# Twenty-five indirect fetches moved from the end of an attention stage into its loop over key tiles

## The reference, cut to what matters

```python
h = jnp.maximum(_layernorm(x, axis=-1), 0.0)
x = x + _L0_gnn_ref(h, qW, kW, vW, src, dst)      # attention over edges, 4 heads
h = jnp.maximum(_layernorm(x, axis=-1), 0.0)
# _L1_gnn_ref: x[tgt] is the row of the edge's own target
gamma = e / denom[tgt]                            # softmax of edge_weight per target
msg = jax.nn.relu(x[tgt] @ Wv + bv) * gamma[:, None]
out = jax.ops.segment_sum(msg, tgt, num_segments=n)
```

## Time and profile before

| what | value |
|---|---|
| median of 3 runs | 1339.63 us (1333.62 to 1341.48) |
| span of the profiled execution | 1334.5 us, 23321 instructions |
| PE busy | 1089.8 us, 82% |
| DVE busy | 974.4 us, 73% |
| ACT busy | 691.7 us, 52% |
| POOL busy | 599.0 us, 45% |
| attention, first to last POOL operation | 414.8 to 865.9 us |

### The profile page before, as it was taken

One profiled execution on the slowest core, in us unless ns is written; L12 is line 12 of the kernel. 1 busy time (PEld: TensorE's weight loads), 2 busy tenths in 40 slices (PEclk: granted clock), 3 DMA queues, 4 the chain that ended last, 5 costly groups with the idle time before them and its releaser, 6 DMA issues.

```text
span 1334.5 us, 23321 instructions
## 1 busy us (share of the span) xinstructions
PE 1089.8 (82%) x8345; PEld 633.6 (47%) x8345; DVE 974.4 (73%) x1600; ACT 691.7 (52%) x903; POOL 599.0 (45%) x343
## 2 busy tenths in 40 slices
PE   3878787787796888888788888837996999999893
PEld 2555554454461222222222222214696987788783
DVE  8677888886575999999999999918556535422466
ACT  7555565555446998999898999800000000000221
POOL 8532533422005998999999989960000000000000
PEclk9888878879796999999999999968997999999996
DMA  0100000000144111111112222110011000000201
GB/s 10 30 33 5 7 7 5 8 17 1 40 129 114 36 44 45 47 48 44 45 35 60 53 51 49 45 44 1 1 37 39 25 14 1 22 14 4 66 28 36
DMA packets 98907, 44.80 MB, mean 34 GB/s; under 512 B 85196, under 2 KB 96716, under 8 KB 98672
## 3 DMA queue, kind: packets, MB, share of 16 engines
q1 hardware_dynamic: 97104, 41.58, 11.8%
q0 software_dynamic: 1696, 1.74, 0.5%
HBM read 30.73 MB, written 12.56 MB: 32 GB/s over the span
## 4 chain that ended last, share of the span: by engine, by line
PE 50%; DVE 25%; issue 11%; ACT 5%; POOL 5%; DMA 2%; another core or an unknown queue 2%; SPq 1%; DVEq 0%; ACTq 0%; POOLq 0%
PE PS L1324 19%; DVE Eb L1150 15%; PE PS L553 10%; PE PS L557 8%; POOL Eb L982 3%; DVE Eb L1144 3%; PE PS L1709 3%; PE PS L1332 2%; ACT Eb L1115 2%; PE PS L1074 2%; PE PS L1064 1%; PE PS L1315 1%; ACT Eb L1117 1%; ACT Eb L1119 1%
## 5 line engine op out<-in xcount | busy, mean ns | idle before, releaser
L982 POOL TENSOR_SCALAR Eb<-Eb 128x1024 f32<-128x1024 f32 (+4 forms) x175 | 431.1, 2485 | 74.1 <-ACT Eb L1119 72.8
L1150 DVE SCALAR_TENSOR_TENSOR Eb<-Eb,PS 128x1024 f32<-128x1024 f32 (+4 forms) x350 | 366.7, 1084 | 16.7 <-ACT Eb L1117 10.5
L1324 PE MATMUL PS<-hs,CT 128*128 128x192 f16 (+3 forms) x2500 | 263.3, 267 | 4.0 <-DVE B L1557 1.8
L1119 ACT ACTIVATE Eb<-PS,small 128x1024 f32<-128x1024 f32 (+2 forms) x263 | 251.5, 997 | 28.0 <-PE PS L1064 24.5
L593 ACT ACTIVATE CT<-PS 128x500 f32 x313 | 183.7, 587 | 142.9 <-PE PS L557 135.1
L553 PE MATMUL PS<-mov,oneS 128*128 128x100 f16 x1565 | 184.6, 231 | 76.1 <-issue 71.0
L1324 PEld LDWEIGHTS PS<-hs,CT 128*128 128x128 f16 (+1 forms) x2500 | 227.5, 99 | 37.7 <-DVE SG L1557 2.7
L553 PEld LDWEIGHTS PS<-mov,oneS 128*128 128x128 f16 x1565 | 146.6, 107 | 157.9 <-issue 113.8
L1064 PE MATMUL PS<-Qb,Kb 96*128 96x512 f16 (+3 forms) x700 | 182.8, 364 | 11.1 <-ACT Eb L1119 7.2
L1074 PE MATMUL PS<-Eb,V 128*25 128x512 f32 (+3 forms) x1400 | 169.9, 558 | 3.4 <-DVE Eb L1150 1.8
L435 DVE TENSOR_TENSOR oneS<-iotaX,KL 128x2560 f16<-128x2560 int16 x80 | 120.1, 1501 | 71.6 <-PE PS L557 69.0
(11 more groups left out here) (258 smaller groups left out, 1006.6 us busy)
## 6 DMA issues: line engine op xcount, KB each, us to landing
Kb<-kd SPq DMA_DIRECT2D x168, 96.0 KB, 2.4
qd<-QH SPq DMA_DIRECT2D x12, 192.0 KB, 2.7
kd<-QH SPq DMA_DIRECT2D x12, 192.0 KB, 3.1
hs<-t_d SPq DMA_DIRECT2D x12, 192.0 KB, 2.5
Qb<-qd SPq DMA_DIRECT2D x4, 384.0 KB, 3.9
CT<-x_d SPq DMA_DIRECT2D x1, 1200.0 KB, 7.6
x_d<-B SPq DMA_DIRECT2D x6, 192.0 KB, 1.9
t_d<-A SPq DMA_DIRECT2D x6, 192.0 KB, 1.8
```

The costliest lines, as they stand in the source:

```text
L982: g.tensor_scalar(e, e, ELO, None, ALU.max).then_inc(S("floored"), 1)
L1119: a.activation(e, ps, ACT.Exp, scale=K.unsc[0:r, :]).then_inc(S("score_read"), 1)
L1150: v.scalar_tensor_tensor(out=e, in0=e, scalar=EHI, in1=cn, op0=ALU.min, op1=ALU.mult).then_inc(S("weighed"), 1)
L1324: m = p.matmul(bank(t % FIRST)[0:r, 0:w], K.CT[:, a, 128 * t:128 * t + r], hs[:, a, :, :].rearrange("p k d -> p (k d)"), start=(a == 0), s ...
```

## The change

`attn_gpsimd` waits for `last_edge` at its head. A fetch is then issued behind POOL's operation of steps 9, 15, 21, ... 153 (tiles 0 to 24 of `gG`), in place of the blocks of 4 at the stage's end and of 8 and 13 in the next. The semaphores and the waits of the readers stay as they were.

```diff
+GAMMA_AT = {6 * t + 9: t for t in range(NT)}
+
+
 def attn_gpsimd(g, K):
     S = K.S
+    g.wait_ge(S("last_edge"), 1)
+
+    def gamma(t):
+        i = [t < b for a, b in X_IN].index(True)
+        g.indirect_dma_start(out=K.gG[:, t:t + 1], out_offset=None, in_=K.gs_d,
+                             in_offset=bass.IndirectOffsetOnAxis(ap=K.endI[:, t:t + 1], axis=0)
+                             ).then_inc(S("gamma_in%d" % i), 16)
+
     for it in range(len(ITS)):
...
                 g.tensor_scalar(e, e, ELO, None, ALU.max).then_inc(S("floored"), 1)
+        if it in GAMMA_AT:
+            gamma(GAMMA_AT[it])
     g.wait_ge(S("floored"), halves("P", len(ITS)))
-    g.wait_ge(S("last_edge"), 1)
-    gammas(g, K, 0)
-
-
-def gammas(g, K, i):
-
-    for t in range(*X_IN[i]):
-        g.indirect_dma_start(out=K.gG[:, t:t + 1], out_offset=None, in_=K.gs_d,
-                             in_offset=bass.IndirectOffsetOnAxis(ap=K.endI[:, t:t + 1], axis=0)
-                             ).then_inc(K.S("gamma_in%d" % i), 16)
...
 def prop_gpsimd(g, K):
     S = K.S
-    gammas(g, K, 1)
-    gammas(g, K, 2)
     for i, (a, b) in enumerate(X_IN):
         g.wait_ge(S("gamma_in%d" % i), 16 * (b - a))
```

## The result

The changed kernel takes 1354.12 us, the median of four runs (1345.97 to 1358.65), the kernel before 1339.03 (four runs, 1333.62 to 1341.48). The ratio is 1.0107, 95% interval 1.0065 to 1.0148: slower by about 1%. 1352.6 us was forecast. The profiled execution of the changed kernel is the fastest of its four, 1345.97 us with a span of 1344.0; so the profiles differ by 9.5 us, the medians by 15.1. The forecast of 13.0 lies between.

The account below looks back on a forecast made before the run. The prediction took POOL and DVE together to bound the attention, with two late hand-overs at the propagation's start. 26.7 - 13.7 = +13.0 us on the median of 1339.6 gave 1352.6 us, range 1338 to 1368.

Parts of the forecast that it names:

- The attention, +26.7: Attention: the 25 fetches, paid in POOL's order, add 26.7 us, with ends of 13 and 38.
- ten steady slots: Attention: ten fetches in stretches where POOL has no gap, 1.5 us each, 15.0 us.
- six of blocks 4 and 5: Attention: six fetches in the steady part of blocks 4 and 5, 1.35 us each, 8.1 us.
- nine near a block's start: Attention: nine fetches close to a block's start, partly swallowed by POOL's gaps, 0.4 us each, 3.6 us.
- The 0.2 us that I put on top for line 1144: Attention: a fetch without a gap costs 1.5 us, not 1.30, as POOL's next operation is stretched by line 1144.
- The meeting I described: Attention: POOL's delayed operation begins inside DVE's line 1144 and takes 3.19 us, 0.43 more than 2.76.
- The stage change, -13.7: From attention to propagation: without the fetches 13.7 us go, 12.1 of late hand-overs and 1.6; ends 0 and 15.3.
- The 12.1 us of hand-overs: Propagation's start: two late hand-overs from PE, to ACT 6.33 and to DVE 5.77 us, go with the fetches.
- The clock's share, 1.6 us: Propagation's start: PE stays warmer at granted clock 1.00, so its first group is 1.6 us shorter.
- 1, that the hand-overs stay: Propagation's start: the late hand-overs have another cause and remain; 1366.3 us, chance 0.25.
- 2, that POOL's idle time swallows more: Attention: POOL's idle time of about 20 us takes up more of the fetches; 1338.4 us, chance 0.16.
- 3, that 1144 and POOL exclude each other: Attention: the fetch or POOL's next operation lasts until line 1144 ends; attention +38, 1363.9 us, chance 0.09.

Follow-up runs that it names:

- experiment 2: The changed kernel with each fetch one step earlier, behind even steps: 1381.08 us, ratio to before 1.0307.
- experiment 8: The changed kernel with a second, spare fetch behind each of the first 24: 1400.66 us, ratio to before 1.0457.
- 1: No fetch at all, against the kernel before: a memset writes 1.0 into gG instead; 1325.96 us, ratio 0.9895.
- 3: The 25 fetches moved to POOL's idle time: 17 in the projection, 6 at the attention's head, 2 behind steps 32 and 82; 1338.09 us, ratio to before 0.9977.
- 4: The changed kernel plus 21 spare fetches into unused columns at the propagation's head: 1369.54 us, ratio to before 1.0233.
- 5: The changed kernel plus 21 spare fetches in the propagation, held back until `lin_read`: 1377.79 us, ratio to before 1.0265.
- 7: The changed kernel plus 21 spare fetches at the propagation's head, 14 tiny memsets behind each, some 3.4 us apart: 1352.29 us, ratio to before 1.0093.
- 9: The kernel before with four tiny memsets ahead of each of the propagation's 21 fetches, 1.80 us apart: 1324.89 us, ratio 0.9889.
- 10: The kernel before with two tiny memsets ahead of each of the propagation's 21 fetches, 1.49 us apart: 1324.76 us, ratio 0.9895.
- 12: The kernel before with six tiny memsets ahead of every third fetch of the propagation: 1325.65 us, ratio 1.0005 to before at 1325.27.
- run 6: The 25 fetches placed singly: 6 in the projection, 2 at the attention's head, 17 at steps beside POOL's gaps; 1337.36 us, ratio to before 0.9972.

## Why the prediction was right, and where not

*What bounds the kernel.* Right: POOL and DVE are bound together, a fetch in POOL's order is paid in full, and neither catches up. The chain's swap from DVE to POOL is the same statement.

*The attention, +26.7.* Measured +24.3. For each slot, the time from the start of POOL's operation three steps ahead to that three steps behind (the last slot reaches to the end of the attention), less the same in before:

| kind | forecast | measured |
|---|---|---|
| ten steady slots | 15.0 (1.5 each) | 12.9 (0.75 to 2.21; six of them 1.24 to 1.29) |
| six of blocks 4 and 5 | 8.1 (1.35 each) | 6.8 (-0.47 to 1.92) |
| nine near a block's start | 3.6 (0.4 each) | 4.6 (-1.15 to 2.25) |

The lower bound held: 1.30 forecast from the earlier trace rows, 1.25 found. The 0.2 us that I put on top for line 1144 was wrong for the steady slots. The meeting I described does happen, but the price falls on the other engine. The timeline of DVE behind the first fetch:

```profile
443.22 1.69 DVE L1147 TENSOR_SCALAR Eb<-Eb 128x1024 f32<-128x1024 f32 x1
444.94 3.54 DVE L1153 SCALAR_TENSOR_TENSOR Eb<-Eb,PS 128x1024 f32<-128x1024 f32 x3
448.86 1.22 DVE L1153 SCALAR_TENSOR_TENSOR Eb<-Eb,PS 128x1024 f32<-128x1024 f32 x1 [0.38 <-POOL Eb L993]
450.00 0.69 DVE L1147 TENSOR_SCALAR Eb<-Eb 128x1024 f32<-128x1024 f32 x1
```

Line 1147 starts 0.08 us ahead of POOL's next operation and takes 1.69 us, not 0.69; POOL's takes its usual 2.77. DVE pays 1.00 us within the 1.25 that POOL is late anyway, and has to wait for POOL 0.38 us a step later. So the 1.00 us lies in DVE's slack and costs nothing. In experiments 2 and 8 it comes to 1.42 us (2.11 less 0.69) behind a POOL operation that is already late, and there it is paid.

*The stage change, -13.7.* Measured -14.9. The 12.1 us of hand-overs are gone, and 1, 3, 4, 5, 7, 9 and 10 show that the fetches made them, with the caution told under 12. The clock's share, 1.6 us, was wrong as a mechanism. Windows of the kernel after, from the first group's copy to the second group's product (columns as in the earlier trace rows):

```profile
907.64:909.93 2.29, 1.57 (x13) 1.15 (x10) 0.00 (x1) 0.69 (x2) 0.00 (x0) 1.00 0.00 0
909.93:914.08 4.15, 0.00 (x0) 0.00 (x0) 3.94 (x18) 0.21 (x1) 0.00 (x0) 0.74 0.00 0
914.08:917.88 3.80, 3.11 (x13) 2.61 (x14) 3.56 (x17) 0.59 (x1) 0.00 (x0) 0.50 0.00 0
```

The granted clock is 1.00 (2.4 GHz) at the first product, which takes 1.15 us in place of 2.02. Then PE stands idle for 4.15 us while DVE normalises the next rows, as in the kernel before, and the clock falls to 0.50 (1.2 GHz). The second group's transposes, product and source sums take 1.10, 2.03 and 6.45 us, and the group 11.9 us (914.08 to 925.99) in place of 11.2: 0.9 gained and 0.7 lost, nearly nothing together. The prediction overlooked that idle stretch.

A gain of 2.7 us that nobody forecast fills the place: the first transposes end 18.8 us behind POOL's last operation (889.29 to 908.09) and not 21.5 (865.93 to 887.39). It can't be put down to the fetches. The five other kernels without a fetch at this place (1, 2, 3, 6, 8) have 19.6 to 21.1, as much as the kernel with two memsets (21.0), which has them. So kernels with no fetch there at all lie 2.3 us apart, and what sets this stretch no run shows. That the term of 13.7 comes so near to 14.9 is in part luck.

*The sum.* By the profiles 24.3 - 14.9 + 0.1 = 9.5 us, by the medians 15.1; 13.0 was forecast. The two errors of the terms, 2.4 and 1.2 us, both lie on the side of too slow; by the profiles the change costs 3.5 us less than forecast, by the medians 2.1 more. The profiled execution of after, with the highest granted clock of its four (0.932 against 0.906 to 0.918), lies 8 us under its median. So the medians' 15.1 is not explained to the microsecond, only within the interval of 1.0065 to 1.0148, and that 13.0 lies so near to it is luck in part as well.

*The rivals.* 1, that the hand-overs stay, is refuted. 2, that POOL's idle time swallows more, is refuted for this placing: the attention grew by 24.3 us, not by under 13.7, and the 3.21 us gap stayed. In the better placing of run 6 it holds in part: 17 fetches cost 8.1 us there, not the 21 of 1.25 each. 3, that 1144 and POOL exclude each other, was given 38 us and 0.09. It didn't happen in the changed kernel; one step aside it did, at +57.3 us. The Trainium skill, "SBUF — State Buffer", section "SBUF: two separate sides", says that between GpSimd's instruction and a VectorE one in a two-port mode, whichever starts first has the shared port pair for its whole length. The runs agree with it in part, as the last section shows; in the row at 443.22 DVE's operation starts 0.08 us ahead of POOL's and is the one that is held.

*What the prediction had no eye for.* The kernel before itself can lie 15 us lower in another sitting. If the changed kernel has one level only, which no run here tested, the same change would cost (1354.1 - 1325.3) / 1325.3, about 2%, an estimate.

## What to carry to other kernels

Work that nobody waits for can still cost: a wait whose releaser the profile can't place, on a kernel with one core, is a thing to chase before any work is moved. Here two tiny dependent instructions between the fetches did what moving them into a full loop did, without the loop's price: 1324.8 us, the best of both kernels and all runs in the sitting where before took 1340.0 (where before itself took 1325.3, a like pause gained nothing). And in a loop where two engines run in lock step, an insertion is priced by the phase into which it pushes the next meeting of the two, not by its length: the same fetch cost 1.25 us behind one step and up to 4 behind the next. Try such a placing one step to either side before you believe its cost.

## What the runs showed of the hardware

**DVE's lower bound and POOL's operation.** In the fourteen traces (before, after, and the experiments) I took every instance of line 1144 (1147 and so on) with 1024 elements that started inside an operation 982 (993 and so on) of POOL or less than 0.1 us ahead of one, 672 in all, and set its duration against the time that was left of that operation:

```
left of POOL's op (us)   instances   duration of the DVE op
2.0 and more             80          left - 1.18 (all 80; 36 of them began just ahead of it)
1.59 to 2.0              22          0.69
1.565 to 1.59            460         0.69 (all 460)
1.54 to 1.565            23          left + 0.55 (all 23), that is 2.11
1.0 to 1.54              2           left + 0.55
under 1.0                85          left + 0.55 (79), 0.69 (5, within the last 0.12 us), one other
```

So DVE's operation is held through the first part of POOL's, can pass at one opening about the middle, and from there on is held until POOL ends and needs 0.55 us more. The steady state of the kernel before comes 1.20 us into POOL's operation and passes each time; between 1.21 and 1.23 us some pass and some don't. Durations of over 2.0 us number none in before and after, 13 of 50 each in experiments 2 and 8, 2 in 6. What shows it in one row is 464.24 above: POOL's operation ends at 465.79, line 1147 at 466.35. Why POOL's operation has an opening, no run shows.

The Trainium skill's page "SBUF — State Buffer" (section "SBUF: two separate sides") has the loser of the shared port pair blocked for the whole of the other's instruction. That fits what begins behind the opening: held until POOL's operation ends (79 of 85). It doesn't fit what begins ahead of it: all 80 are released with POOL's operation still running, and end 1.18 us before it does. And at the opening both engines get through side by side; the whole tuned loop lives from that.

**PE's completion under close fetches.** With fetches 1.25 us apart a signal from PE was seen 5.8 to 10.5 us late in the rows shown, in the propagation (before, 4, 5) and in the projection (3, where the next ones on ACT were over 12 us late); signals of ACT in the same stretches were not (in before, ACT's copy ends at 894.31 and PE starts at 894.37). The first three fetches of a run did no harm in before: PE's completions at 867.8 and 869.1 us came at once. As matmul ends are modelled, no run shows whether PE's work itself ended late or its signal alone. What is full or held there no run shows, nor what sets the kernel's level for a sitting.

**A fetch's own time depends on what DVE does beside it.** It is 1.03 to 1.05 us in all 25 slots of the changed kernel and 0.94 or 0.95 in 24 of 25 at the stage change of the kernel before, with 0.16 to 0.30 of issue ahead. Where one of DVE's operations on SBUF tensors runs across its start it can take longer: ten of the second fetches of experiment 8 took 1.16 to 1.32 us with line 1152 begun 0.20 to 0.35 us ahead of them, one fetch of experiment 2 took 1.51 with line 1147 begun 0.07 ahead.
